# One tile of x1 moved from VectorE to GpSimd, a new order in the dense steps, and no wait for scatters in the edge steps

## The chip, the core and the metric

One core of a Trainium2 chip runs the whole kernel: TensorE (PE), VectorE (DVE), ScalarE (ACT), GpSimd (POOL) and SyncE (SP, used for its DMA queue). The metric is the time of one execution on the device in microseconds (us), less is better.

## The reference, cut to what matters

There are N = 50000 nodes with 128 features in `x`, and 12500 edges (98 tiles of 128 edges) sorted by destination.

```python
# layer 0 (GraphSAGE-like, max over edges)
pooled = relu(layer_norm((x[src] * (1 + softplus(coeff) * w[:, None])) @ pool_w + pool_b))
agg    = maximum(segment_max(pooled, dst), 0)
h      = relu(layer_norm(concat([x, agg]) @ final_w + final_b))
x1     = layernorm(x + h)
# layer 1 (relational graph convolution, 8 bases, mean over edges)
msg    = x1[src];  aggs[b] = segment_sum(msg * comp[edge_type][:, b], dst)
out    = concat([agg_b / max(deg, 1) for b], x1) @ weight + bias
return layernorm(x1 + out)
```

For a node without an incoming edge `agg` is zero, so its x1 and its output need its own row alone.

## The kernel before, in words

**Dense and edge groups.** A group is 4 tiles of 128 rows. The first 98 groups ("dense") are all rows of x: each gets x1 and an output as if it had no edges. Then 25 groups ("edge") redo the rows that are destinations of edges, with `agg`, and their x1 rows are scattered over the dense ones in `x1_table`. After that, phase C goes through the 98 tiles of edges in 25 units: it gathers x1 rows of the sources, multiplies by coefficients, applies the bases, sums by destination, normalises, and scatters the final rows into `out`.

**Steps.** A software pipeline of 130 steps, written out by hand on each engine. In step s a dense group g is at stage s - g: 0 load and transpose, 1 first matmul, 2 scaling by gamma, 3 beta and residual, 4 x1, 5 transpose of x1, 6 root matmul, 7 output. Beside it each step takes one tile of edges (from step 5 on) through gathers, a matmul and a running maximum (`scanned`), so that `agg` is ready for the edge groups. An engine does its stages of a step in program order; counting semaphores (`dve_x`, `act_x`, `pe_c`, ...) tie the engines together. Up to step 103 (`c < EDGE_ORDER`) one order holds, behind it another.

**VectorE in a dense step:** moments of the last statistics (L1084, L1085: two operands in SBUF), residual `h = max(h, 0) + x` (L1119: one instruction of 512 elements, both operands in SBUF, waits for `pool_b`), `spread` (L1090, waits for L1084), variance (L1095), bn_stats (L1107) four times, reciprocal (L1143), the scan (L1153), gamma scaling `scaled` (L1171, four times), the fourth tile of x1 (`first_layer`, L1202), `pooled_scaled` (L1164), the output (L1182).

**GpSimd in a dense step:** adds beta to the whole group (L461, waits for `dve_t`, that is for `scaled` of the step before), issues the gather of rows x[dst] (`gather_dst`, L431), scales the source rows by the edge's weight (`scale_src`, L452, 128x128), issues the gather of x[src] (`gather_src`, L438). In the edge steps it issues four scatters a group (L486).

**ScalarE in a dense step:** copy of x1 transposed (L775), square root of the reciprocals (`roots`, L782), squares of the root layer's output for its variance (`rooted`, L767), three tiles of x1 (`first_layer`, L805), squares of the first layer (`squares`, L767), the copy of the transposed rows (L827).

**TensorE in a dense step:** transposes of x1 (L539), root bias (L548), root matmuls (L554), first bias (L578), first matmuls (L586), transposes of rows (L565), the transpose of `pooled` (L600), the pooling layer (L610, L611). In `first_bias` it waits, in edge groups, until the scatters of the group five before have landed (`x1_scattered`): the brake of the diff below.

**SP's queue in a dense step** stores x_dst, loads the next group (after the residual), stores x1 (after `act_x` and `dve_x`), and stores the output.

Of the kernel before, what the change touches and what calls it, by code (L numbers as in the profile page):

```python
# [16 lines left out]
P = 128  # L17
CH = 4
# [55 lines left out]
def gnn_kernel(nc, x, src_cols, dst_cols, dst_next_cols, dst_rows, dst_prev_rows, type_line,  # L74
# [35 lines left out]
    with ExitStack() as ctx:  # L110
# [92 lines left out]
        def banks(a, n):  # L203
# [13 lines left out]
                 "dve_t", "dve_te", "pool_b", "apart_stored", "agg_ready", "act_e", "scaled", "e_ready", "dve_v", "dve_x", "act_x", "dve_o", "pe_c", "pe_cp", "act_c", "dve_scan", "pe_d",  # L217
# [71 lines left out]
        def _(sp):  # L289
# [44 lines left out]
            def step(s):  # L334
# [41 lines left out]
                if is_dense(c, 4):  # L376
                    sp.wait_ge(S["act_x"], s - 3)
                    sp.wait_ge(S["dve_x"], s - 3)
# [28 lines left out]
        def _(pool):  # L407
# [45 lines left out]

            def step(s):
# [17 lines left out]
                if is_tile(s, -3):  # L472
                    need(pool, S["pe_a"], s)
                    gather_src(s + 3 - LATE)
                if is_group(s, 4) and not is_dense(s, 4):
# [8 lines left out]
                    pool.wait_ge(S["dve_x"], s - 3)  # L484
# [39 lines left out]
        def _(pe):  # L524
# [3 lines left out]
            def step(s):  # L528
# [4 lines left out]
                def turned():  # L533
                    if is_group(c, 5):
                        pe.wait_ge(S["act_x"], s - 4)
                        pe.wait_ge(S["dve_x"], s - 4)
# [31 lines left out]
                def first_bias():  # L568
                    if c == 1:
                        pe.wait_ge(S["setup_dve"], 1)  # L570
                    if is_group(c, 1):
                        d = c - 1 - DENSE - LEAD
                        if d >= 0:
                            pe.wait_ge(x1_scattered[d % LEAD], 16 * CH * (d // LEAD + 1))
# [39 lines left out]
                if c < EDGE_ORDER:  # L614
                    turned()
                    root_bias()
                    rooted()
                    first_bias()
# [117 lines left out]
        def _(act):  # L736
# [25 lines left out]
            def step(s):  # L762
# [14 lines left out]
                def roots():  # L777
                    if 2 <= c <= GROUPS + 3:
                        act.wait_ge(S["dve_q"], s - 1)
                        if is_group(c, 5):  # L780
                            act.wait_ge(S["act_x"], s - 4)
                        nc.scalar.activation(st[:, 7, :], st[:, 6, :], ACT.Sqrt, scale=float(D)).then_inc(S["act_q"], 1)  # L782
# [58 lines left out]
                if c < EDGE_ORDER:  # L841
                    turned()
                    roots()
                    rooted()
                    first_layer()
# [49 lines left out]
        def _(dve):  # L895
# [202 lines left out]
            def step(s):  # L1098
# [24 lines left out]
                residual()  # L1123
                if stats:
                    own.need(first)
                    spread_at = spread(RES, TOP)

# [65 lines left out]
                def first_layer():  # L1193
                    if is_group(c, 4):
                        if is_dense(c, 4):
                            need(dve, S["pe_c"], s - 5)
                        else:
                            dve.wait_ge(S["pe_b"], s - 3)
                        if is_dense(c, 4) and is_dense(c, 6):
                            dve.wait_ge(x1_stored[b], 16 * since(c, 4 + b, 2))  # L1200
# [12 lines left out]
                if c < EDGE_ORDER:  # L1213
# [7 lines left out]
                    scaled()  # L1221
                    first_layer()
                    stats_of(2)
                    pooled_scaled()
# [145 lines left out]
```

## Time and profile before

| | |
|---|---|
| median of 3 runs | 882.5 us (880.93 to 883.58) |
| the profiled execution | 882.3 us, its span 880.5 us |
| busy share of the span | PE 90%, DVE 88%, ACT 68%, POOL 80% |
| TensorE's mean granted clock | 0.957 of full speed |
| dense steps | about 10 to 480 us of the span |
| edge steps | about 480 to 628 us |
| phase C | from 628 us |

The span runs from the first to the last instruction. A row of the trace gives start and duration of an instruction (or of several alike in a row, with xN), its line, what it writes and reads, and in brackets the idle time of its engine before it with what ended it ("issue": nothing that the profile shows). Starts can overlap the end of the instruction before, since the engines pipeline.

### The profile page before, as it was taken

How to read it: one execution, taken by the hardware profiler on the slowest of the kernel's cores; microseconds unless marked ns; L12 is line 12 of the kernel's file. 1: busy time of each engine (PE TensorE's matmuls, PEld its weight loads, DVE VectorE, ACT ScalarE, POOL GpSimd, SP SyncE). 2: the span in 40 equal slices, each digit the busy share in tenths (PEclk: the TensorE clock that was granted, in tenths of full speed). 3: DMA queues.
4: the chain of work that ended last, by engine and by line, in shares of the span. 5: the costliest groups of instructions: out<-in, count | busy, mean ns of one | idle time of the engine just before them, and what ended most of it. 6: DMA issues, size and time to landing. Idle time of an engine off the chain costs nothing.

```text
span 880.5 us, 17875 instructions
## 1 busy us (share of the span) xinstructions
PE 793.3 (90%) x4519; PEld 553.4 (63%) x4519; DVE 775.1 (88%) x2703; ACT 601.5 (68%) x2887; POOL 703.4 (80%) x703
## 2 busy tenths in 40 slices
PE   4699999999999999999999999997499998989760
PEld 3577777777777777777777787775345544434340
DVE  6999999999999999999999999986179999999780
ACT  4699999999999999999999988885202121111130
POOL 2599899899899899899898577776677777777777
PEclk9899999999999999999999999999589999999895
DMA  4366676666666666676666534444187887878711
GB/s 115 107 221 221 214 241 219 214 219 221 210 219 222 209 221 218 207 222 221 211 219 199 172 123 124 134 149 144 48 291 280 321 285 287 303 271 303 270 47 46
DMA packets 90699, 179.84 MB, mean 204 GB/s; under 512 B 17161, under 2 KB 36018, under 8 KB 84326
## 3 DMA queue, kind: packets, MB, share of 16 engines
q1 hardware_dynamic: 73414, 147.26, 50.1%
q0 software_dynamic: 15744, 30.96, 11.2%
q8 instruction: 37, 0.61, 0.3%
q10 hardware_dynamic: 1440, 0.50, 0.3%
q14 instruction: 64, 0.52, 0.2%
HBM read 109.02 MB, written 70.91 MB: 204 GB/s over the span
## 4 chain that ended last, share of the span: by engine, by line
PE 56%; POOL 23%; issue 9%; DVE 6%; ACT 3%; DMA 3%; ACTq 0%; POOLq 0%; DVEq 0%
PE ps L586 13%; PE ps L554 13%; POOL out_rows L431 11%; POOL rows L438 11%; PE ps L565 6%; PE ps L539 5%; PE ps L611 4%; PE ps L578 4%; PE ps L548 4%; PE ps L600 3%; PE ps L610 2%; POOL x_table L486 2%; PE ps L589 2%; DMA x_table<-agg_all,scat_x 1%; ACT junk L767 1%
## 5 line engine op out<-in xcount | busy, mean ns | idle before, releaser
L767 ACT ACTIVATE junk<-ps 128x128 bf16<-128x128 f32 x884 | 233.0, 287 | 21.1 <-PE ps L589 12.3
L767 ACT ACTIVATION_READ_ACCUMULATOR junk<-ps 128x1 f32 x884 | 193.6, 219 | 0.0
L719 PE MATMUL ps<-agg_all,w_cen 128*128 128x512 f32 (+1 forms) x400 | 178.0, 599 | 3.1 <-DVE agg_all L1271 2.5
L431 POOL DMA_INDIRECT x_dst<-in_x,dst_i x98 | 153.5, 1566 | 14.9 <-issue 4.5
L586 PE MATMUL ps<-w_cen,xT 128*128 128x128 f32 x984 | 157.8, 292 | 1.4 <-ACT xT L827 1.4
L461 POOL TENSOR_TENSOR work<-work,vec_raw 128x512 f32<-128x512 f32 x98 | 124.6, 1272 | 35.4 <-DVE work L1171 24.7
L586 PEld LDWEIGHTS ps<-w_cen,xT 128*128 128x128 f32 x984 | 127.9, 195 | 30.2 <-issue 27.9
L554 PE MATMUL ps<-w_cen,work 128*128 128x128 f32 x984 | 146.2, 293 | 0.0
L1271 DVE TENSOR_TENSOR agg_all<-coefs,ps 128x1024 f32<-128x1024 f32 x98 | 117.7, 1210 | 29.7 <-PE ps L705 18.3
L554 PEld LDWEIGHTS ps<-w_cen,work 128*128 128x128 f32 x984 | 122.3, 196 | 28.8 <-issue 28.8
L1107 DVE BATCH_NORM_STATS2 bn<-work 128x6 f32<-128x128 f32 x492 | 133.0, 276 | 0.7
L719 PEld LDWEIGHTS ps<-agg_all,w_cen 128*128 128x128 f32 x400 | 76.3, 196 | 88.5 <-issue 88.2
L486 POOL DMA_INDIRECT x_table<-agg_all,scat_x x98 | 94.2, 961 | 40.6 <-issue 27.4
L431 POOL DMA_INDIRECT out_rows<-work,scat_i x98 | 97.3, 993 | 29.9 <-issue 29.3
L438 POOL DMA_INDIRECT rows<-x_table,src_i x98 | 93.6, 955 | 31.8 <-issue 29.0
L438 POOL DMA_INDIRECT rows<-in_x,src_i x98 | 96.7, 987 | 18.7 <-issue 15.6
L1171 DVE SCALAR_TENSOR_TENSOR work<-ps,st,vec_raw 128x128 f32<-128x128 f32 x392 | 108.5, 336 | 2.2 <-ACT st L782 1.1
L881 ACT ACTIVATE st<-st 128x4 f32<-128x4 f32 x25 | 5.1, 206 | 148.2 <-DVE st L1307 147.8
L805 ACT ACTIVATE work<-work,st 128x128 f32<-128x128 f32 x294 | 97.9, 417 | 0.1
L565 PE MATMUL ps<-ident,rows 128*128 128x128 f32 x590 | 86.2, 276 | 7.6 <-DMA rows<-in_x 6.6
L827 ACT COPY xT<-ps 128x640 f32<-128x640 f32 (+1 forms) x123 | 85.7, 697 | 0.6 <-PE ps L565 0.6
L775 ACT COPY work<-ps 128x512 f32<-128x512 f32 x123 | 77.9, 633 | 1.7 <-PE ps L539 1.6
(147 smaller groups left out, 1399.8 us busy)
## 6 DMA issues: line engine op xcount, KB each, us to landing
coefs<-coef_line SPq DMA_DIRECT2D x49, 1024.0 KB, 7.4
rows<-in_x SPq DMA_DIRECT2D x97, 256.0 KB
x_table<-work SPq DMA_DIRECT2D x97, 256.0 KB, 2.1
out_rows<-outb SPq DMA_DIRECT2D x97, 256.0 KB, 2.1
x_dst_table<-x_dst SPq DMA_DIRECT2D x98, 64.0 KB
rows<-x_dst_table SPq DMA_DIRECT2D x24, 256.0 KB
apart<-apart_line SPq DMA_DIRECT2D x14, 224.0 KB
x_dst<-in_x,dst_i POOLq DMA_INDIRECT x98, 4.0
```

Source lines behind the costliest of these rows:

```text
L431: return pool.indirect_dma_start(*args, bounds_check=last_node, oob_is_err=False)
L438: return pool.indirect_dma_start(rows_of, None, table, by(columns, t))
L461: pool.tensor_tensor(h, h, vec_raw[:, BET_F:BET_F + 1, :].broadcast_to([P, CH, D]), ALU.add).then_inc(S["pool_b"], 1)
L486: pool.indirect_dma_start(x1_table[:, :], by(scat_x, d * CH + m), x1_tile(s - 4, m), None) \
L554: last = pe.matmul(Y[b][:, cols(m, m + 1)], x1T[:, b, m, :], w_cen[:, W_ROOT, :], start=False, stop=True, skip_group_check=True)
L565: last = pe.transpose(XT[:, cols(m, m + 1)], rows[:, slot, m, :], ident[:, :])
L586: last = pe.matmul(H[1 - b][:, cols(m, m + 1)], xT[:, 1 - b, m, :], w_cen[:, W_TOP, :], start=False, stop=is_dense(c, 1), skip_group_check ...
L719: last = pe.matmul(MT[b][:, 0:n * D], w_cen[:, W_BASE + m, :], prod[:, b, m, 0:n, :].rearrange("p t d -> p (t d)"), start=(m == 0), stop=( ...
L767: last = nc.scalar.activation(junk[:, kind * CH + m, :], bank[:, cols(m, m + 1)], ACT.Square, accum_out=power[:, b, 1, TOP + kind * CH + m ...
L1107: own.mark(dve.bn_stats(bn[:, RES + m, :], hn[:, (c - 3) % SLOTS, m, :]))
L1171: last = dve.scalar_tensor_tensor(hn[:, (c - 2) % SLOTS, m, :] if is_dense(c, 2) else h, h, st[:, 7, TOP + m:TOP + m + 1], vec_raw[:, GAM_ ...
L1271: dve.tensor_tensor(prod[:, b, half, two, :], coefs[:, p % COEF_SLOTS, :, half, :].rearrange("p t m d -> p m t d"), GX[c % len(GX)][:, col ...
```

## The change

1. `fourth_x1`, new on GpSimd: in dense steps tile 3 of x1 is made there, as a multiply of 128x128 by a broadcast column, behind `gather_src`; it signals `pool_x`. SP's store, TensorE's transposes and ScalarE's `roots` wait for `pool_x` in dense groups. VectorE's `first_layer` is left for edge groups alone, and `dve_x` counts only these.
2. Order in steps up to 103. TensorE: `first_bias` ahead of `rooted`. ScalarE: `first_layer` ahead of `rooted`. VectorE: the residual behind `spread` (this in all steps), and `pooled_scaled` ahead of `first_layer` and the third bn_stats.
3. TensorE's wait for `x1_scattered` in `first_bias` is gone.

```diff
@@ SP
-                    sp.wait_ge(S["dve_x"], s - 3)
+                    sp.wait_ge(S["pool_x"], s - 3)
@@ GpSimd
+            def fourth_x1(s):
+                c, b = s, s % 2
+                if is_dense(c, 4):
+                    pool.wait_ge(S["act_q"], s - 1)
+                    need(pool, S["pe_c"], s - 5)
+                    if is_dense(c, 6):
+                        pool.wait_ge(x1_stored[b], 16 * since(c, 4 + b, 2))
+                    pool.tensor_tensor(x1_tile(c - 4, X1_ACT), hn[:, (c - 4) % SLOTS, X1_ACT, :],
+                                       st[:, 7, RES + X1_ACT:RES + X1_ACT + 1].broadcast_to([P, D]), ALU.mult) \
+                        .then_inc(S["pool_x"], 1)
...
                     gather_src(s + 3 - LATE)
+                fourth_x1(s)
...
-                    pool.wait_ge(S["dve_x"], s - 3)
+                    pool.wait_ge(S["dve_x"], s - 3 - DENSE)
@@ TensorE
-                        pe.wait_ge(S["dve_x"], s - 4)
+                        if is_dense(c, 5):
+                            pe.wait_ge(S["pool_x"], s - 4)
+                        else:
+                            pe.wait_ge(S["dve_x"], s - 4 - DENSE)
...
-                        d = c - 1 - DENSE - LEAD
-                        if d >= 0:
-                            pe.wait_ge(x1_scattered[d % LEAD], 16 * CH * (d // LEAD + 1))
...
                     root_bias()
+                    first_bias()
                     rooted()
-                    first_bias()
                     first_layer()
@@ ScalarE
                         act.wait_ge(S["dve_q"], s - 1)
+                        if is_dense(c, 5):
+                            act.wait_ge(S["pool_x"], s - 4)
...
                     roots()
+                    first_layer()
                     rooted()
-                    first_layer()
                     squares()
@@ VectorE
-                residual()
                 if stats:
                     own.need(first)
                     spread_at = spread(RES, TOP)
+                residual()
...
-                    if is_group(c, 4):
-                        if is_dense(c, 4):
-                            need(dve, S["pe_c"], s - 5)
-                        else:
-                            dve.wait_ge(S["pe_b"], s - 3)
-                        if is_dense(c, 4) and is_dense(c, 6):
-                            dve.wait_ge(x1_stored[b], 16 * since(c, 4 + b, 2))
+                    if is_group(c, 4) and not is_dense(c, 4):
+                        dve.wait_ge(S["pe_b"], s - 3)
...
                     scaled()
+                    pooled_scaled()
                     first_layer()
                     stats_of(2)
-                    pooled_scaled()
                     stats_of(3)
```

## Rows read from the trace of the kernel before

**Rows 1.** Busy time by stretch: us; PE, PEld, DVE, ACT, POOL busy; clock; DMA
```profile
300.00:400.00 100.00, 98.72 (x657) 74.56 (x655) 96.85 (x383) 96.80 (x507) 89.99 (x86) 1.00 0.68 216
```

**Rows 2.** The chain of waits from 400 to 410 us: start, us, what
```profile
by line: PE ps L586 25.9%; PE ps L554 21.8%; PE ps L565 10.9%; PE ps L578 9.5%; PE ps L539 8.7%; PE ps L611 8.3%; PE ps L548 6.3%; PE ps L600 6.0%; PE ps L610 3.2%; issue 1.0%
...
404.55 0.32 PE ps L578
...
406.85 0.16 PE ps L610
```

**Rows 3.** GpSimd in order of time, at steps 12 and 98: start, us, engine, line
```profile
59.91 0.99 POOL L438 DMA_INDIRECT rows<-in_x,src_i  x1 [0.16 <-issue]
60.92 1.28 POOL L461 TENSOR_TENSOR work<-work,vec_raw 128x512 f32<-128x512 f32 x1
...
467.29 1.27 POOL L461 TENSOR_TENSOR work<-work,vec_raw 128x512 f32<-128x512 f32 x1
```

**Rows 4.** GpSimd and VectorE in order of time, one steady step
```profile
404.21 0.41 POOL L452 TENSOR_TENSOR rows<-rows,e_scale 128x128 f32<-128x128 f32 x1
...
404.77 0.99 POOL L438 DMA_INDIRECT rows<-in_x,src_i  x1 [0.16 <-issue]
...
405.72 0.27 DVE L1202 TENSOR_SCALAR work<-work,st 128x128 f32<-128x128 f32 x1
...
405.88 1.27 POOL L461 TENSOR_TENSOR work<-work,vec_raw 128x512 f32<-128x512 f32 x1
405.91 0.28 DVE L1107 BATCH_NORM_STATS2 bn<-work 128x6 f32<-128x128 f32 x1
...
407.30 1.59 POOL L431 DMA_INDIRECT x_dst<-in_x,dst_i  x1
407.30 0.68 DVE L1119 SCALAR_TENSOR_TENSOR work<-work,rows 128x512 f32<-128x512 f32 x1
...
408.19 0.47 DVE L1095 SCALAR_TENSOR_TENSOR st<-power,st 128x13 f32<-128x13 f32 x1
```

**Rows 5.** The same two engines in an early step, in order of time
```profile
46.93 1.28 POOL L461 TENSOR_TENSOR work<-work,vec_raw 128x512 f32<-128x512 f32 x1
...
47.93 0.31 DVE L1084 TENSOR_TENSOR st<-bn 128x4 f32<-128x4 f32 x1
...
48.25 0.69 DVE L1119 SCALAR_TENSOR_TENSOR work<-work,rows 128x512 f32<-128x512 f32 x1
48.37 1.46 POOL L431 DMA_INDIRECT x_dst<-in_x,dst_i  x1 [0.16 <-issue]
```

**Rows 6.** The same, in step 6 and in an edge step
```profile
32.78 1.02 POOL L431 DMA_INDIRECT x_dst<-in_x,dst_i  x1 [0.17 <-issue]
...
33.29 0.69 DVE L1119 SCALAR_TENSOR_TENSOR work<-work,rows 128x512 f32<-128x512 f32 x1
33.89 0.16 DVE L1090 SCALAR_TENSOR_TENSOR st<-st 128x4 f32<-128x4 f32 x1
...
34.15 0.17 DVE L1095 SCALAR_TENSOR_TENSOR st<-power,st 128x13 f32<-128x13 f32 x1
...
552.41 0.96 POOL L486 DMA_INDIRECT x_table<-agg_all,scat_x  x1 [0.30 <-issue]
552.44 0.43 DVE L1029 TENSOR_TENSOR w_cen<-w_cen,row_mean 128x256 f32<-128x256 f32 x1
```

**Rows 7.** Waits from 495 to 630 us (total us, times, longest), and one scatter
```profile
POOL x_table L486 <- DVE agg_all L1202: 8.5, 7, 3.6
...
PEld ps L578 <- DMA x_table<-agg_all,scat_x: 5.0, 3, 3.9
...
608.29 0.96 POOL L486 DMA_INDIRECT x_table<-agg_all,scat_x  x1 [3.60 <-DVE agg_all L1202]
```

**Rows 8.** Phase C on GpSimd: its first gather, and the gathers as a group
```profile
628.47 0.98 POOL L438 DMA_INDIRECT rows<-x_table,src_i  x1 [2.24 <-DMA x_table<-agg_all,scat_x]
...
L438 POOL DMA_INDIRECT rows<-x_table,src_i x98 | 93.6, 955 | 31.8 <-issue 29.0
```

More of the change, by code:

```diff
@@ L216, in gnn_kernel @@
                  "setup_dve", "bases_dve", "base_sums", "bases_ready", "soft_dve", "soft_act", "pe_a", "act_a", "pe_b", "pe_e", "act_h", "dve_q", "act_q",
-                 "dve_t", "dve_te", "pool_b", "apart_stored", "agg_ready", "act_e", "scaled", "e_ready", "dve_v", "dve_x", "act_x", "dve_o", "pe_c", "pe_cp", "act_c", "dve_scan", "pe_d",
+                 "dve_t", "dve_te", "pool_b", "apart_stored", "agg_ready", "act_e", "scaled", "e_ready", "dve_v", "dve_x", "pool_x", "act_x", "dve_o", "pe_c", "pe_cp", "act_c", "dve_scan", "pe_d",
                  "act_y", "act_o", "dve_own", "deg_dve", "deg_pe", "root_centred", "col_sums", "root_ready", "c_own", "pe_g", "act_g",
```

## The prediction

> **What bounds the kernel now.** I read the stretches first. Through the dense steps TensorE, VectorE and ScalarE are each busy 97 to 99% of the time and GpSimd 90%, all at the full TensorE clock [rows 1]. Then the chain of waits for two steps: TensorE's own instructions from end to end, with 1% of "issue" [rows 2]. The spacing of the beta addition on GpSimd (L461) gives the period: from step 12 (60.92 us) to step 98 (467.29 us) [rows 3] there are 86 steps in 406.4 us, 4.725 us each. Then one step in order of time [rows 4]. It shows that four loops close at nearly the same length:
> - TensorE: 4.72, of which 0.05 is "issue" (1.0% of 10 us, two steps) [rows 2]; it lies just before L600, the transpose that needs VectorE's `pooled`.
> - ScalarE: 3.2% idle [rows 1], so 4.58 of work and 0.15 of gaps.
> - GpSimd, back to back: L461 1.27, gap 0.15, L431 1.59, gap 0.03, L452 0.41, gap 0.16, L438 0.99, gap 0.02 [rows 3, 4] = 4.62.
> - VectorE with GpSimd: scaled, then L461, then the residual L1119, then statistics, then scaled again.
>
> After the dense steps the bound is GpSimd's issue of indirect DMAs. Scatters take 0.96 us each with 0.30 between; of their waits, 8.5 us in 7 places are for VectorE's x1 [rows 7]. From the first gather of phase C (628.47) on, GpSimd issues 98 gathers and 98 scatters with about 0.30 us between them [rows 8], 252 us that begin when the last x1 row has landed. So the end moves by what the dense and edge steps give or take.
>
> **The change, part by part.**
>
> *The fourth tile on GpSimd.* VectorE loses L1202: from its start to that of the next instruction 0.19 us (405.72 to 405.91). GpSimd gains one multiply of 128x128 with a broadcast column, the form of L452: 0.41 us, plus 0.02 for the gap as between L438 and L461. It stands behind L438, and ahead of the next L461. Its inputs are there when its turn comes (L438 ends at 405.76): L1202 needed the same three semaphores and ran at 405.72. It would be ready near 406.2. Those who wait for it are the store on SP's queue (with the output store, the copy of x_dst and the next load behind it), TensorE's transposes of the next step, and ScalarE's next root, ahead of which the change adds a wait; all of them come after the next L461 has started (405.88), and before, the store waited for ScalarE's three tiles, which end later than L1202. So each costs nothing as long as GpSimd keeps pace. A price for the three waits isn't shown; bounds are 0 (L461's gap of 0.02 behind a wait) and 0.16 (the gap before L438, which waits too); I take 0, the nearest row being a vector operation like it. As the rows of before stand GpSimd would then need 4.62 + 0.43 = 5.05 us a step, more than 4.72. The question is therefore whether the 1.59 us of L431 stay.
>
> *Why L431 takes 1.59 us.* The same gather took 1.02 us at 32.78, where the residual L1119 started 0.51 us after it; at 48.37, where L1119 had started 0.12 us before it, 1.46; in the steady steps both start within 0.01 us and it takes 1.59 [rows 4 to 6]. In each slow case it ends 1.58 to 1.59 us after L1119's start: it waits out L1119 (two operands in SBUF) and then does its whole work. I counted 94 gathers slowed so, and none where L1119 started more than 0.01 us after L431. Rows of L1119 starting between 0.01 and 0.51 after don't exist.
>
> *The new order of VectorE.* The residual moves behind L1084, L1085 and the spread L1090, which waits for L1084. Without L1202, VectorE reaches L1084 0.19 us earlier, while L461 still runs, and is held there: at 47.93 L1084 took 0.31 instead of 0.15, and ended 0.03 after L461 (48.21) [rows 5]. From its end a dependent instruction needs 0.10 to 0.14 us (L1090 ends 34.05, L1095 starts 34.15 [rows 6]), and the next one follows 0.07 later. So, counted from the end of L461, L1090 starts at 0.13 to 0.17 and L1119 at 0.20 to 0.24, while L431 starts at 0.15: L1119 comes 0.05 to 0.09 us after L431, where before it came with it. Does L431 get through? For: the scatter L486 at 552.41, with a two-operand VectorE instruction starting 0.03 after it, took its plain 0.96 [rows 6]. Against: L1090, also with two operands, starts at L431's own time, and L1119 follows it closely. I take "gets through": L431 1.02, so GpSimd's floor is 4.62 - 0.57 + 0.43 = 4.48 us, and it is not the bound. The other end is a full stall: L431 ends 0.22 + 1.59 after L461, GpSimd's floor is 1.27 + 1.81 + 0.03 + 0.41 + 0.16 + 0.99 + 0.02 + 0.41 + 0.02 = 5.12.
>
> The page "SBUF — State Buffer" of the Trainium skill (section "SBUF: two separate sides") says that the port pair which VectorE and GpSimd share is an exclusive lock, that a VectorE operation with two SBUF inputs contends for it against a GpSimd operation that reads SBUF, and that whoever starts first keeps it for the whole instruction while the other blocks. The stalls above agree with the first two. The last would have L431, once first, hold L1119 up for its whole length; the row at 33.29 speaks against that (L1119 took 0.69 in the middle of a gather), but it makes a rival below.
>
> *What is then late next.* VectorE's loop through L461 is 4.72 now. L1119 would come 0.07 later behind L461 (0.22 for 0.15), but L1095 sooner behind L1119: 0.60 (33.29 to 33.89) instead of 0.86 (to 34.15) [rows 6]: 4.53. And L1095 took 0.47 at 408.19 beside the stalled gather, 0.17 at 34.15 [rows 4, 6]: if that goes too, 4.23. TensorE: `pooled` comes right behind scaled, ahead of two instructions it stood behind, so L600's 0.05 goes; the two bias matmuls now stand side by side. A bias matmul of 512 columns (L578) is 0.32 of the chain, one of 128 columns (L610) 0.16 [rows 2], so 384 columns are 0.16, and some 0.11 of each is not columns; side by side saves 0 to 0.11, and TensorE's floor is 4.56 to 4.67. ScalarE: 4.58 plus gaps that may stay (0.04 to 0.11), as its order only swaps two blocks. I take 4.65 for the period, bounds 4.58 and 4.69. Sum: 86 x (4.65 - 4.725) = -6.5 us, between -12.5 and -3.
>
> *No brake in the edge steps.* TensorE's first bias waited for scatters 5.0 us in 3 places, the longest 3.9 [rows 7]; it is followed by GpSimd's wait of 3.60 at 608.29 and one of 0.87 later. Less the 0.30 that any gap has, these two are 3.9 us. The other 1.1 us of the brake come before; they shorten GpSimd's later waits by as much. Together -5.0. ScalarE makes the x1 of the first edge group ahead of its four squares instead of behind them, which may bring the first scatter forward by up to 1.0, the four squares' time; I take half. Bounds: -1 (another engine paces those steps) and -6.4 (all of 8.5 less 7 x 0.30). Taken -5.5. The clock dips to half in the idle stretches around 600 and 620 us; the first would go too, inside the same sum.
>
> *Sum.* -6.5 - 5.5 = -12.0 against the profiled execution's own 882.3 us (span 880.5), which is 0.2 under the median of 882.5: 870.4 us.
>
> **The rivals.**
> 1. *L431 still stalls behind the residual* (slower). Place: every dense step. Price: 5.12 - 4.725 = 0.395 x 86 = +34.0, some +2 in steps 5 to 12, -5.5 at the edge: 912.8, give or take 5. It decides as soon as GpSimd's floor passes 4.7, that is when more than about a third of the steps stall. For: the distance is under 0.1 us and L1090 sits on L431's start. Against: 552.41.
> 2. *A part of the steps stalls*, or the three waits of the new tile cost their 0.16 each: GpSimd's period between 4.70 and 5.0, so 876 to 900.
> 3. *The gather holds the residual.* By that page's rule, worked out in this kernel: L1119 would start at L431's end (1.17 after L461), VectorE's loop is 4.23 to 4.53 and 0.95 more: 5.18 to 5.48, dense +39 to +65, time 916 to 942. Against it: L1119 at 33.29, and L1029 at 552.44, which took 0.43 us beside a scatter.
> 4. *The dense steps don't move* (another loop stands at 4.72) and only the brake counts: 877.
>
> **How the numbers follow.** Forecast, with 4: 0.57. Rival 1: 0.23. Rival 2: 0.15. Rival 3: 0.05. About 0.3% (2.6 us) can be told from no change. Faster: 0.57 and half of rival 2 = 0.65. Same: 0.06. Slower: 0.29. The likeliest case's own range is 865 to 879. The range of 8 in 10 has to reach over rival 2 into rival 1: 865 to 911.
>
> **What would show it.** Right: L461 spaced 4.6 to 4.7; L431 near 1.02 us with L1119 starting 0.05 to 0.09 after it; L1084 stretched to L461's end; the new multiply 0.41; L600 without a wait; no wait of L578 for a scatter; the last scatter less than 1.0 us late after the one before. Wrong: L431 of 1.6 us or more and a GpSimd that is busy without a gap, period 5.1; then rival 1. A residual that takes over 1 us is rival 3. A period of 4.72 with TensorE's chain unbroken says that the bias matmuls and L600 gave nothing.

## The result, and the profile after

The changed kernel takes 861.86 us (median of 3 runs, 861.31 to 862.27), the kernel before 882.5: ratio 0.9767, interval 0.9742 to 0.9793. A second series later gave 861.71 against 882.79. The forecast was 870.4 with a range of 865 to 911: the direction was right, the gain is 20.6 us where 12.0 were expected, and the time lies below the range. The profiled execution's span is 860.5 us, 20.0 less than before (clock 0.956, before 0.957).

Where the 20.0 us come from, by landmarks on GpSimd (the beta addition, L461 before and L472 now; the scatters, L486 and L498; the first gather of phase C, L438):

| stretch | before | after | difference | forecast |
|---|---|---|---|---|
| start to step 12 | 60.92 | 60.23 | -0.7 | - |
| steps 12 to 98 (86 steps) | 406.37 | 388.23 | -18.1 | -6.5 |
| step 98 to step 100 | 10.01 | 10.24 | +0.2 | - |
| step 100 to the first scatter | 17.69 | 18.77 | +1.1 | -0.5 |
| first scatter to phase C | 133.48 | 131.01 | -2.5 | -5.0 |
| phase C | 252.0 | 252.0 | 0 | 0 |

The steps that answer to [rows 3]; from them the period is 388.23 / 86 = 4.514 us (before 4.725):

```profile
60.23 1.27 POOL L472 TENSOR_TENSOR work<-work,vec_raw 128x512 f32<-128x512 f32 x1
...
448.46 1.27 POOL L472 TENSOR_TENSOR work<-work,vec_raw 128x512 f32<-128x512 f32 x1
```

The stretch from 300 to 400 us, columns as in [rows 1]:

```profile
300.00:400.00 100.00, 96.84 (x688) 75.03 (x688) 96.74 (x377) 99.24 (x535) 91.21 (x111) 1.00 0.73 227
```

Before, TensorE stood highest with 98.7%; now ScalarE does, with 99.2%. The chain of waits from 400 to 410 us, which was all TensorE's [rows 2], now has no piece of it:

```profile
by line: ACT junk L779 41.5%; ACT work L819 19.8%; ACT xT L841 17.5%; ACT junk L831 12.1%; ACT st L796 6.0%; ACT work L787 4.6%; issue 4.4%; ACTq L53 0.5%
```

And a steady step on GpSimd and VectorE, to lay beside [rows 4] (L1098, L1104, L1133 and L1109 are the old L1084, L1090, L1119 and L1095; L461 is now the new multiply):

```profile
403.37 1.28 POOL L472 TENSOR_TENSOR work<-work,vec_raw 128x512 f32<-128x512 f32 x1
...
404.45 0.23 DVE L1098 TENSOR_TENSOR st<-bn 128x4 f32<-128x4 f32 x1
...
404.71 0.17 DVE L1104 SCALAR_TENSOR_TENSOR st<-st 128x4 f32<-128x4 f32 x1
...
404.79 0.72 DVE L1133 SCALAR_TENSOR_TENSOR work<-work,rows 128x512 f32<-128x512 f32 x1
404.79 1.04 POOL L431 DMA_INDIRECT x_dst<-in_x,dst_i  x1
...
405.66 0.17 DVE L1109 SCALAR_TENSOR_TENSOR st<-power,st 128x13 f32<-128x13 f32 x1
...
407.42 0.42 POOL L461 TENSOR_TENSOR work<-work,st 128x128 f32<-128x128 f32 x1
```

The gather took 1.04 us where it took 1.59, although the residual starts with it again, at 404.79, as it did before. The variance behind it took 0.17 where [rows 4] had 0.47, and the new multiply 0.42.

### The profile page after: what moved, and what is told of

Read it like the earlier page. It is cut to its first block, busy times and chain, and to the rows that moved or that the text cites. A ratio compares the mean times of both kernels' runs of the same rounds, so it can differ in the third digit from the quotient of the medians.

```text
span 860.5 us, 17875 instructions
## 1 busy us (share of the span) xinstructions
PE 767.1 (89%) x4519; PEld 542.2 (63%) x4519; DVE 756.1 (88%) x2605; ACT 593.2 (69%) x2887; POOL 692.1 (80%) x801
## 4 chain that ended last, share of the span: by engine, by line
DVE 31%; POOL 23%; ACT 22%; issue 11%; PE 10%; DMA 2%; DVEq 0%; SPq 0%; ACTq 0%; POOLq 0%
POOL out_rows L431 11%; POOL rows L438 10%; ACT junk L779 9%; DVE work L1185 7%; ACT work L819 5%; DVE bn L1121 5%; DVE work L1133 4%; DVE outb L1196 4%; ACT xT L841 3%; PE ps L569 2%; PE ps L598 2%; ACT junk L831 2%; PE ps L601 2%; ACT st L796 2%; DVE agg_all L1167 2%
## 5 line engine op out<-in xcount | busy, mean ns | idle before, releaser
L779 ACT ACTIVATE junk<-ps 128x128 bf16<-128x128 f32 x884 | 227.7, 280 | 11.7 <-PE ps L601 9.1
L779 ACT ACTIVATION_READ_ACCUMULATOR junk<-ps 128x1 f32 x884 | 189.4, 214 | 0.0
L569 PEld LDWEIGHTS ps<-w_cen,work 128*128 128x128 f32 x984 | 122.8, 196 | 47.7 <-issue 46.9
L598 PE MATMUL ps<-w_cen,xT 128*128 128x128 f32 x984 | 150.8, 286 | 0.6 <-ACT xT L841 0.6
L569 PE MATMUL ps<-w_cen,work 128*128 128x128 f32 x984 | 146.8, 294 | 0.0
L472 POOL TENSOR_TENSOR work<-work,vec_raw 128x512 f32<-128x512 f32 x98 | 124.6, 1271 | 22.3 <-DVE work L1185 19.5
L598 PEld LDWEIGHTS ps<-w_cen,xT 128*128 128x128 f32 x984 | 131.4, 199 | 7.4 <-issue 5.5
L1121 DVE BATCH_NORM_STATS2 bn<-work 128x6 f32<-128x128 f32 x492 | 126.1, 277 | 3.6 <-DVE work L1133 0.9
L498 POOL DMA_INDIRECT x_table<-agg_all,scat_x x98 | 94.1, 960 | 37.9 <-issue 27.5
L438 POOL DMA_INDIRECT rows<-x_table,src_i x98 | 93.6, 955 | 31.8 <-issue 29.6
L431 POOL DMA_INDIRECT x_dst<-in_x,dst_i x98 | 102.4, 1045 | 14.4 <-issue 2.3
L1185 DVE SCALAR_TENSOR_TENSOR work<-ps,st,vec_raw 128x128 f32<-128x128 f32 x392 | 110.3, 344 | 2.8 <-ACT st L796 1.8
L438 POOL DMA_INDIRECT rows<-in_x,src_i x98 | 96.7, 987 | 18.3 <-issue 15.7
```

What stands on the lines that cost most here:

```text
L431: return pool.indirect_dma_start(*args, bounds_check=last_node, oob_is_err=False)
L438: return pool.indirect_dma_start(rows_of, None, table, by(columns, t))
L472: pool.tensor_tensor(h, h, vec_raw[:, BET_F:BET_F + 1, :].broadcast_to([P, CH, D]), ALU.add).then_inc(S["pool_b"], 1)
L569: last = pe.matmul(Y[b][:, cols(m, m + 1)], x1T[:, b, m, :], w_cen[:, W_ROOT, :], start=False, stop=True, skip_group_check=True)
L598: last = pe.matmul(H[1 - b][:, cols(m, m + 1)], xT[:, 1 - b, m, :], w_cen[:, W_TOP, :], start=False, stop=is_dense(c, 1), skip_group_check ...
L779: last = nc.scalar.activation(junk[:, kind * CH + m, :], bank[:, cols(m, m + 1)], ACT.Square, accum_out=power[:, b, 1, TOP + kind * CH + m ...
```

## The experiments

Two theories on the dense steps. **A**: the stalled gather was what mattered; it frees GpSimd for the new multiply, and everything that puts the residual ahead of the gather costs that back. **B**: TensorE never bound at 4.725; what bounds after the change is ScalarE, and the orders of TensorE and ScalarE are worth little. For the edge steps: the brake was worth the held scatters, or it was cover for something else.

Four of them (`e_residual`, `e_pe_order`, `e_act_order`, `e_brake`) ran on one chip on which everything behind the dense steps is slower (the kernel before took 971.6 us there, 966.35 to 976.92; from the first scatter to phase C it is 182 to 184 us there, on the others 129 to 136). So of them only ratios and the dense steps are used; these had their usual pace there. The changed kernel itself did not run on that chip. Kernels with the same dense steps (the two runs of the changed one, `e_brake`, `e_brake_again`, `e_edge_residual`) have periods from 4.514 to 4.527, so 0.01 us of period means nothing. On the others the kernel before took 882.8 to 883.4.

**e_residual**: residual back ahead of the spread, in dense steps.
```diff
+                if c < EDGE_ORDER:
+                    residual()
                 if stats:
                     own.need(first)
                     spread_at = spread(RES, TOP)
-                residual()
+                if c >= EDGE_ORDER:
+                    residual()
```


> The changed kernel with VectorE's residual back ahead of the spread in the dense steps (the edge steps keep the new order). Theory A (what frees GpSimd's gather of x_dst is that the residual no longer follows the two moments directly): the gather takes 1.46 to 1.6 us again, GpSimd's floor is 4.93 to 5.07, +0.42 to +0.56 us a step, +36 to +48 us, 898 to 910. Theory B (VectorE, freed of the fourth tile, is early enough in any order): the gather stays at 1.04 and the time within 2 us of 861.9.

982.89 us, ratio 1.0133 (1.0061 to 1.0205), period 4.887. The residual starts 0.12 us ahead of the gather, which takes 1.49:

```profile
302.84 0.69 DVE L1133 SCALAR_TENSOR_TENSOR work<-work,rows 128x512 f32<-128x512 f32 x1
302.96 1.49 POOL L431 DMA_INDIRECT x_dst<-in_x,dst_i  x1 [0.16 <-PE ps L554]
303.45 0.16 DVE L1104 SCALAR_TENSOR_TENSOR st<-st 128x4 f32<-128x4 f32 x1
303.74 0.44 DVE L1109 SCALAR_TENSOR_TENSOR st<-power,st 128x13 f32<-128x13 f32 x1
```

With the extra multiply GpSimd now sets the period: its five instructions follow each other after 1.44 + 1.51 + 0.57 + 1.01 + 0.36 = 4.89 us (medians), none of them with a wait for another engine. One line moved costs 0.37 us a step against the changed kernel (4.887 for 4.514), nearly twice what the whole change gained.

**e_tile_alone**: the kernel before with only the tile moved to GpSimd (old orders, brake); cut to the call.
```diff
                     gather_src(s + 3 - LATE)
+                fourth_x1(s)
```


> The kernel before with the fourth tile on GpSimd and nothing else: old orders, brake kept. Both theories: the residual starts 0.12 us before the gather, which takes 1.46 to 1.5 us; GpSimd needs 1.27 + 0.15 + 1.48 + 0.03 + 0.41 + 0.16 + 0.99 + 0.02 + 0.41 + 0.03 = 4.95 us a step, so +0.2 x 86 = +19 us against the kernel before. If VectorE is late instead and the gather gets through, the period is 4.5 to 4.7.

897.92 us, ratio 1.0167 (1.0147 to 1.0187), period 4.877, gather 1.49: the same picture on the ordinary chip. This is the first rival's mechanism, at +13 us in the dense steps (86 x 0.152) and not +34.

**e_resid_only**: the kernel before with the residual behind the spread, nothing else.
```diff
-                residual()
                 if stats:
                     own.need(first)
                     spread_at = spread(RES, TOP)
+                residual()
```


> The kernel before with one line moved: VectorE's residual behind the spread (the fourth tile stays on VectorE, the brake and all other orders stay). Theory A (the old bound of 4.725 us was the loop of GpSimd and VectorE with the gather stalled behind the residual; TensorE only kept step with it): the gather drops to about 1.04 and the period to 4.5 to 4.6, which is -11 to -19 us. Theory B (TensorE bounded the steps at 4.72 and its bias order had to change too): the gather drops, the period stays at 4.65 to 4.72, at most -6 us.

870.85 us, ratio 0.9858 (0.9839 to 0.9877), period 4.580. The gather takes 1.02, the residual starts 0.12 after it. So this single move gives 12.5 of the 18.1 us of the dense steps (86 x 0.145). TensorE is busy 99.75% here:

```profile
300.00:400.00 100.00, 99.75 (x679) 77.27 (x679) 97.12 (x395) 97.62 (x523) 80.43 (x88) 1.00 0.71 221
```

That is not its floor. The transpose of `pooled` (L600) starts 0.68 us after the five transposes ahead of it (median, 0.54 to 0.96), where in `e_pe_order` below, with the same order on TensorE, 0.56 is enough for a step of 4.52. One of these steps, with 0.70:

```profile
403.24 0.71 PE L565 MATMUL ps<-ident,rows 128*128 128x128 f32 x5
403.94 0.30 PE L600 MATMUL ps<-ident,pooled 128*128 128x128 f32 x1
```

ScalarE's squares wait for TensorE's L554 (2.3 us in 100) and VectorE's variance for ScalarE's L817 (2.5), so that the three wait for each other in turn. Which link would have to give for less than 4.58 was not tested.

**e_order_alone**: the new orders and no brake, the fourth tile left on VectorE, behind `pooled_scaled`; cut to VectorE's part.
```diff
                     scaled()
+                    pooled_scaled()
                     first_layer()
                     stats_of(2)
-                    pooled_scaled()
                     stats_of(3)
```


> The changed kernel with the fourth tile made by VectorE again: new orders on all engines, no brake. Theory A (GpSimd's own work of 4.51 us bounds the changed kernel): GpSimd falls to 4.07 and the period follows the next engine, VectorE at about 4.55 (4.37 busy and 0.19) or ScalarE at 4.48: between 4.48 and 4.6, within 3 us of the changed kernel or up to 7 us slower. Theory B (the tile on GpSimd is what brings the gain): period back near 4.7, +17 us against the changed kernel.

954.17 us, ratio 1.0805 (1.0784 to 1.0826), period 5.579: much slower, which I had not expected. The cause is one instruction:

```profile
300.15 1.26 POOL L461 TENSOR_TENSOR work<-work,vec_raw 128x512 f32<-128x512 f32 x1 [1.28 <-DVE work L1168]
300.24 1.25 DVE L1199 TENSOR_SCALAR work<-work,st 128x128 f32<-128x128 f32 x1
```

The tile on VectorE (L1199) starts 0.09 us after the beta addition and takes 1.25 us instead of 0.28 (0.27 to 0.28 in every other kernel that has it there): it is held until the addition ends. All that VectorE has to do behind it comes a microsecond late.

**e_tile_first**: the same, but the tile directly behind the four scalings, so that it starts ahead of the addition.
```diff
                     scaled()
-                    pooled_scaled()
                     first_layer()
+                    pooled_scaled()
                     stats_of(2)
```


> The changed kernel with the fourth tile on VectorE directly behind the scaling (as before), pooled behind it; the other new orders stay, no brake. Tests why the same order with the tile behind pooled took 5.58 us a step. Theory A (behind pooled it starts 0.09 us after GpSimd's beta addition and is held until its end, 1.25 us for 0.28; directly behind scaled it starts ahead of it): the tile takes 0.28 again, period 4.5 to 4.6, whole time 860 to 869. Theory B (VectorE can't carry the tile in the new order whatever its place): period over 5, above 900.

861.65 us (860.52 to 862.25), ratio 0.9751 (0.9728 to 0.9775), period 4.514. The same tile now starts ahead of the addition and takes its plain time:

```profile
403.13 0.28 DVE L1199 TENSOR_SCALAR work<-work,st 128x128 f32<-128x128 f32 x1
...
403.29 1.27 POOL L461 TENSOR_TENSOR work<-work,vec_raw 128x512 f32<-128x512 f32 x1 [0.48 <-DVE work L1168]
```

It is as fast as the change, with GpSimd at 82% instead of 91%. Moving the tile to GpSimd is therefore one way to keep it out of the addition's way, and not the source of the gain. Against `e_resid_only` (4.580) this kernel has the new orders of TensorE and ScalarE and `pooled_scaled` ahead of the third bn_stats: together they are the remaining 0.066 us a step.

**e_pe_order** and **e_act_order**: TensorE's, then ScalarE's old order in the changed kernel.
```diff
                     root_bias()
-                    first_bias()
                     rooted()
+                    first_bias()
```


> The changed kernel with TensorE's old order (root matmuls ahead of the first bias). Theory A (TensorE was the bound at 4.72 us a step and its floor fell by some 0.2 because the two bf16 bias matmuls now share one switch; GpSimd and ScalarE at 4.51 bound the steps now): the floor returns to about 4.65, so +0.14 x 86 = +12 us, 874, with TensorE at 99% busy. Theory B (TensorE was never the bound, the old chain only ran through it): within 1 us of 861.9, period 4.51.

```diff
                     roots()
-                    first_layer()
                     rooted()
+                    first_layer()
```


> The changed kernel with ScalarE's old order (squares of the root layer ahead of x1). Theory A (ScalarE is a bound now at 99% busy and the new order took 0.1 us of its gaps and waits out of a step): period up by 0.05 to 0.1 and +4 to +9 us, 866 to 871. Theory B (the order of two blocks on ScalarE is worth nothing where GpSimd alone is the bound): within 1 us of 861.9; x1 comes 1.0 us later and the store with it, which nobody waits for.

949.31 (ratio 0.9798, 0.9733 to 0.9862) and 946.99 (0.9774, 0.9703 to 0.9845); periods 4.526 and 4.497. With its old order TensorE is busy 99.88% of the time at 4.526 us a step. So the work that before filled 4.725 us fits into 4.526, and no effect of its new order on the period can be told from the spread of like kernels. Theory B, for the kernel with the tile on GpSimd.

**e_pool_light** and **e_act_light**: less work on one engine. In the first, GpSimd scales one column of 128 of the source rows (L452, tiles 4 to 89); in the second ScalarE leaves one of the four squares of the root layer out in steps 12 to 97. These parts of the computation are missing.
```diff
-                pool.tensor_tensor(r, r, e_scale[:, t:t + 1].broadcast_to([P, D]), ALU.mult).then_inc(S["scaled"], 1)
+                w = 1 if 4 <= t < 90 else D
+                pool.tensor_tensor(r[:, 0:w], r[:, 0:w], e_scale[:, t:t + 1].broadcast_to([P, w]), ALU.mult).then_inc(S["scaled"], 1)
```


> The changed kernel; GpSimd's scaling of source rows works on 1 column instead of 128 for edge tiles 4 to 89, so part of that result is left out. It frees some 0.26 us of GpSimd a step, floor 4.25. Theory A (GpSimd's 4.51 alone bounds the step): the period falls to ScalarE's 4.48 or a little above it, -0.02 to -0.03, -2 us. Theory B (GpSimd isn't the bound): 4.51 stays. If VectorE and GpSimd together made the 4.51, it falls below 4.45.

```diff
-                        squared(Y[b], 1).then_inc(S["act_y"], 1)
+                        squared(Y[b], 1, CH - 1 if 12 <= c < 98 else CH).then_inc(S["act_y"], 1)
```


> The changed kernel with one of ScalarE's four squares of the root layer left out in steps 12 to 97, 0.25 us of ScalarE a step, so the variance of a fourth of those rows is left out. Theory A (GpSimd bounds): period 4.51, unchanged. Theory B (ScalarE, 99% busy, bounds): the period falls to below 4.45, -5 us or more.

860.91 (0.9745, 0.9717 to 0.9773) and 854.2 (0.9669, 0.964 to 0.9698); periods 4.513 and 4.441. GpSimd is not the bound, ScalarE is. Relieved, it hands over after 0.07 us, to VectorE, which has no idle time left:

```profile
300.00:400.00 100.00, 98.51 (x696) 76.00 (x697) 100.00 (x383) 97.59 (x498) 91.81 (x113) 1.00 0.74 230
```

GpSimd has no slack there either: its own five spacings add up to 1.43 + 1.07 + 0.57 + 1.01 + 0.36 = 4.44. Which of the two stops at 4.44 these runs don't tell.

**e_nudge**: the kernel before with one more small addition on VectorE between L1085 and the residual, its result unused.
```diff
                 own.mark(dve.tensor_tensor(power[:, par, 1, a:b], bn[:, a:b, 2], bn[:, a:b, 5], ALU.add))
+                own.mark(dve.tensor_tensor(st[:, 3, a:b], bn[:, a:b, 2], bn[:, a:b, 5], ALU.add))
```


> The kernel before with one more small addition on VectorE (128x4, the form of L1085, its result unused) between L1085 and the residual: the residual starts some 0.06 to 0.10 us later, and what stands ahead of it is still a two-operand instruction of the kind that stood there. Theory 'only the distance counts: a gather that has begun is let through': the gather takes 1.02 to 1.05, the period 4.58 to 4.65, the time 870 to 876, although an instruction was added. Rival 'what stands ahead of the residual counts (in the kernel after the spread, in before the moments)': the gather still takes 1.5 to 1.6 and the time is 882 to 890.

899.22 us, ratio 1.0183 (1.0162 to 1.0204), period 4.881. Half of each theory: the gather takes 1.02, the residual starting 0.12 after it, so the distance does decide there; but the time is neither's. The step got 0.156 us longer, although GpSimd got 0.57 us back:

```profile
400.18 0.15 DVE L1085 TENSOR_TENSOR power<-bn 128x4 f32<-128x4 f32 x1
400.26 0.18 DVE L1086 TENSOR_TENSOR st<-bn 128x4 f32<-128x4 f32 x1
400.36 0.68 DVE L1120 SCALAR_TENSOR_TENSOR work<-work,rows 128x512 f32<-128x512 f32 x1
400.97 0.37 DVE L1091 SCALAR_TENSOR_TENSOR st<-st 128x4 f32<-128x4 f32 x1
401.46 0.28 DVE L1096 SCALAR_TENSOR_TENSOR st<-power,st 128x13 f32<-128x13 f32 x1
```

The two small instructions behind the residual are stretched (0.37 and 0.28), as one of them was in [rows 4] (L1095, 0.47). VectorE has no waits in such a step. So in the kernel before it was VectorE that set the period, and its loss beside the gather is the same whether the gather gets through or not. Theory A in its plain form ("a free gather is the gain") falls with this run. What the new order gains, by the spacings in the table below, is that the spread is no longer behind the residual.

**e_brake**, **e_brake_again** (the changed kernel with the brake, on the slow and on an ordinary chip) and **e_no_brake** (the kernel before without it).
```diff
                     if is_group(c, 1):
+                        d = c - 1 - DENSE - LEAD
+                        if d >= 0:
+                            pe.wait_ge(x1_scattered[d % LEAD], 16 * CH * (d // LEAD + 1))
                         need(pe, S["dve_t"], s - 2)
```


> The changed kernel with TensorE's wait for scatters put back in the edge steps; nothing else. Theory A (read from the two traces: the last 28 scatters follow back to back now, where before there were 3.3 + 0.57 us of gaps behind the brake's 3.9 us hold): +3.9 us, so about 866, with the hold of nearly 4 us back at the fourth last group. Theory B (the dense steps' end and not the brake set the edge steps' time, the brake is worth nothing): within 1 us of 861.9. My prediction's term of 5.0 to 5.5 us would give 867.

954.32, ratio 0.9816 (0.9752 to 0.988); period 4.527. No run on that chip differs from it by the brake alone, so it says nothing on the brake.

> The kernel after with TensorE's wait for x1_scattered back in first_bias, once more, on a chip where the edge steps may run at their usual speed. Theory 'the brake cost what the two held waits show' (3.60 and 0.87 us less 0.30 each in the trace of before, none of it in the trace of after): 3 to 5 us slower than the kernel after, so 865 to 867. Rival 'another engine paces those steps, the brake was cover for VectorE's x1': within 1 us of it, 861 to 863. Dense period 4.51 in both.

865.74 us (864.93 to 866.1), ratio 0.980 (0.978 to 0.982).

> The kernel before with that wait left out and nothing else changed. By the first theory 3 to 5 us under the kernel before, 878 to 880; by the rival within 1 us of it. Dense period 4.725 in both, and the first scatter where before had it.

879.48 us, ratio 0.9956 (0.9939 to 0.9974). The brake costs 865.74 - 861.7 = 4.0 us in the one and 883.41 - 879.48 = 3.9 in the other, and 4.0 to 4.1 in both by the stretch from the first scatter to phase C (135.10 against 131.0; 133.48 against 129.43). The waits from 470 to 612 us; first the changed kernel with the brake, where GpSimd waits 4.7 us longer for VectorE's x1:

```profile
POOL x_table L498 <- DVE agg_all L1214: 15.1, 11, 4.1
...
PEld ps L593 <- DMA x_table<-agg_all,scat_x: 5.0, 3, 3.8
```

and the changed kernel:

```profile
POOL x_table L498 <- DVE agg_all L1211: 10.4, 9, 4.1
```

**e_edge_residual** and **e_tile_first_act**, looking for a better version: the old place of the residual in edge steps (the code below), and `e_tile_first` with ScalarE's old order.
```diff
+                if c >= EDGE_ORDER:
+                    residual()
                 if stats:
                     own.need(first)
                     spread_at = spread(RES, TOP)
-                residual()
+                if c < EDGE_ORDER:
+                    residual()
```


> The changed kernel with the old order of residual and spread in the edge steps alone (from step 104). Theory A (there the spread's wait for its moments stands in VectorE's way for 0.1 to 0.15 us in every step that VectorE bounds, and TensorE's first bias waits for the residual): up to -2 us in 25 steps, 860. Theory B (edge steps are bound by TensorE and the scatters): within 0.5 us of 861.8.

> The new order without the brake, the fourth tile on VectorE directly behind the four scalings (which took 861.65), and ScalarE in its old order (which gave a period of 4.497 where the kernel after has 4.514). If ScalarE's order is worth that here too, 86 x 0.017 = 1.5 us: 860.2, less what a later first edge group costs (up to 1.0). If the fourth tile's place matters more, no change from 861.7.

861.34 us (859.77 to 862.73; 0.9745, 0.9718 to 0.9772) can't be told from the change. The other took 870.36 (0.9845, 0.9822 to 0.9869), period 4.605: ScalarE's old order, which in `e_act_order` gave 4.497, costs 0.09 a step here. So the orders are worth little only with the tile on GpSimd. Why it is so was not settled. ScalarE waits there for L554 (1.9 us in 100) and VectorE for ScalarE's L814 (2.0), neither of which `e_tile_first` has.

**after_again**: the changed kernel once more, beside `e_resid_only`.

> The changed kernel as it is, as the reference for the runs beside it: period of the dense steps 4.51 us, gather of x_dst 1.04 us, whole time 0.977 of the kernel before.

861.71 us, ratio 0.9756 (0.9737 to 0.9775), period 4.514. No version beats the change by more than its uncertainty, except the one that leaves work out.

## Why the prediction was right and wrong

**What bounds: the step that failed.** It said that four loops close near 4.72 us and took TensorE for the first of them. Busy shares of 97 to 99% fitted each. Only VectorE had no slack; GpSimd's beta addition came 0.12 us behind the gather and not 0.02, being released by VectorE's `scaled`, and TensorE waited for VectorE's `pooled`. The wait stood just before L600, where I saw it, but as 0.05 us. The rows of before show the start of L600 0.75 us after that of L565:

```profile
405.80 0.71 PE L565 MATMUL ps<-ident,rows 128*128 128x128 f32 x5
406.55 0.30 PE L600 MATMUL ps<-ident,pooled 128*128 128x128 f32 x1
```

In `e_pe_order`, with the same order of TensorE and no such wait, it is 0.56:

```profile
404.15 0.71 PE L580 MATMUL ps<-ident,rows 128*128 128x128 f32 x5
404.71 0.30 PE L612 MATMUL ps<-ident,pooled 128*128 128x128 f32 x1
```

Five transposes have a modelled length of 0.71 in both, so that most of the wait lay under the modelled end. Over the steady steps the medians are 0.77 and 0.56: the wait was 0.21 us. TensorE's floor in its old order was 4.52 (`e_pe_order`: 4.526 at 99.88%) and not the 4.67 from which I worked, so the bounds of the period rested on 0.15 us that weren't there. Nor was the chain of waits a proof that TensorE bound: from 300 to 400 us of `e_act_order` it is TensorE's from end to end too (2.9% "issue"), at a period of 4.497, where TensorE could do its work in 4.22 (below).

**ScalarE: the term that was mis-sized.** I took 96.8% x 4.725 = 4.57 (4.58 in the prediction) for its work, plus gaps. Worked out alike, 99.24% x 4.514 = 4.48, and the gaps are 0.03. The same instructions are recorded shorter: the squares 281 against 290 ns, the three x1 tiles 391 against 418 each (stretches of 100 us of both kernels). They don't follow each other any faster: a square and its read take 0.25 us from start to start in both kernels, the three tiles 0.88 and 0.89. What shrank is a wait: the square root (L782, L796 after) starts 0.73 us after the start of the copy ahead of it before and 0.48 after, while the copy's recorded length is 0.65 and 0.66 (medians). The rows of one step before, then of one after:

```profile
403.59 0.65 ACT L775 COPY work<-ps 128x512 f32<-128x512 f32 x1
404.31 0.21 ACT L782 ACTIVATE st<-st 128x13 f32<-128x13 f32 x1
```
```profile
401.36 0.66 ACT L787 COPY work<-ps 128x512 f32<-128x512 f32 x1
401.84 0.29 ACT L796 ACTIVATE st<-st 128x13 f32<-128x13 f32 x1
```

So ScalarE's slack before was 0.25 us and not 0.15, and a busy share multiplied by the period is no floor of an engine's work. These two errors, both on the high side, put the forecast at 4.65 with bounds 4.58 to 4.69, where 4.514 came: 86 x 0.136 = 11.7 us. That is more than the whole miss of 8.5; the difference went back at the edge, below.

**VectorE's loop: right within the bounds.** I had 4.53, or 4.23 if the stretched variance got its plain time. In `e_act_light`, where VectorE waits for nothing, it is 4.44. The variance did become plain (0.17 at 405.66), but where ScalarE doesn't hold the step, it is stretched again. The spacings of VectorE in the median of some 48 steps show where it gained (all other instructions between: before 3.30, of which L1202 is 0.19, in `e_act_light` 3.11):

| from the first of the moments to | before | e_nudge | e_resid_only | e_act_light |
|---|---|---|---|---|
| the residual | 0.15 | 0.26 | 0.28 | 0.39 |
| the variance | 1.04 | 1.36 | 1.01 | 1.05 |
| behind the variance | 1.43 | 1.56 | 1.18 | 1.33 |

**The gather gets through: right, its reason wrong.** 1.04 us instead of 1.59 came, but not the distance of 0.05 to 0.09. L1084 (now L1098) was stretched to the end of the addition, as said; L1104 followed 0.03 after L1098's end and not 0.13, so the residual starts -0.02 to 0.00 from the gather, where by my rule it should have stalled. `e_resid_only`, `e_nudge` and `e_tile_first` have +0.12 to +0.13 and 1.02; `e_residual` and `e_tile_alone` have -0.12 and 1.49. Between them lies a tie that the records, to 0.01 us, don't resolve: before 0.00 (-0.01 to 0.01) and 1.59, `e_no_brake` +0.01 and 1.59, after -0.01 and 1.04. What decides in a tie is open. The forecast was lucky here.

**GpSimd's floor: right within 0.04.** 4.48 was forecast. The spacings of after add up to the period (1.42 + 1.08 + 0.57 + 1.01 + 0.44 = 4.51), but the last, from the new multiply to the next addition, is 0.36 in `e_residual`, `e_tile_alone` and `e_act_light`: 0.08 of it is a wait for VectorE, and the floor is 4.44. `e_pool_light` shows too that GpSimd doesn't set the period.

**The multiply and its three waits: right**, 0.41 us and nothing measurable (`e_tile_first` has neither and takes the same time). I missed what the move was worth in this order: left behind `pooled_scaled`, the tile would have run under the beta addition at a loss of 92 us (954.17 - 861.7).

**TensorE's order: the term was too small.** I had 0 to 0.11, a floor of 4.56 to 4.67; TensorE itself gained 0.30. By medians of the spacing in steady steps, the first of the two bias matmuls, now side by side, is followed after 0.23 us where each was followed after 0.31, the eight root matmuls after 0.99 (1.09) and the eight first matmuls after 0.89 (1.00):

```profile
404.89 0.39 PE L563 MATMUL ps<-root_bias,ones 3*128 3x512 bf16 x1
405.12 0.37 PE L590 MATMUL ps<-bias,ones 3*128 3x512 bf16 x1
405.43 1.16 PE L569 MATMUL ps<-w_cen,work 128*128 128x128 f32 x8
406.42 1.06 PE L598 MATMUL ps<-w_cen,xT 128*128 128x128 f32 x8
407.31 0.71 PE L580 MATMUL ps<-ident,rows 128*128 128x128 f32 x5
```

With 0.56 ahead of the transpose of `pooled` that is a floor of 4.22, from 4.52. The period shows none of it, since other engines bound; the transpose just waits longer than before (0.84 in place of 0.56), where I had forecast no wait.

**The brake: mechanism right, size off.** The two held waits were priced at 3.9 us, and 3.9 to 4.1 were measured. The 1.1 us that I added for its earlier, shorter waits didn't come: the longer gaps between scatters ahead of the two held ones are the same with the brake (0.60, 0.60, 0.95, 0.94, 0.55, 1.47 us before) and without it (0.61, 0.60, 0.94, 0.95, 0.57, 1.45 in `e_no_brake`). Nor did the half microsecond at the start: the profiled execution lost 1.1 there. That part is the execution's, not the kernel's. TensorE's clock fell to half for some 3.4 us (columns as in [rows 1]):

```profile
466.00:467.40 1.40, 0.67 (x4) 0.46 (x5) 1.38 (x6) 1.40 (x3) 0.00 (x0) 1.00 0.83 263
467.40:470.80 3.40, 3.40 (x19) 3.40 (x18) 3.25 (x12) 2.42 (x13) 1.86 (x3) 0.52 0.55 146
```

In `after_again` it stayed at 1.00 there, and the stretch from step 100 to the first scatter is 17.14 instead of 18.77, 0.55 less than before: so the first scatter does come half a microsecond forward when the clock holds. It doesn't reach phase C. From the first scatter on, the changed kernel needs 131.0 where `e_no_brake` needs 129.4, and from step 100 to phase C `after_again` takes 148.2 and `e_no_brake` 147.1. Of the 1.6 us `e_edge_residual` gives back 0.6 (130.4); the rest is open.

**Rival 1**: 912.8 was too dear. Its period is 4.88 (`e_tile_alone`), not 5.12: the gather, with the residual 0.12 ahead, ends 0.15 + 1.49 after the addition and not 0.22 + 1.59, which is 0.17 less, and the multiply with its gap takes 0.36 where 0.43 was put; together 0.24. **Rival 2** did not come: the gather took 1.04 to 1.05 in every steady step, and the three waits cost nothing measurable. **Rival 3** stays without support: the residual took 0.68 to 0.73 in every kernel whose gather ran beside it. In `e_order_alone` it took 0.91, but there it starts behind the gather's end and lies beside the scaling of the source rows (L452). **Rival 4** is refuted: the dense steps moved by 18.1 us.

## What to carry to other kernels

When all engines are 97 to 99% busy, find the one whose instructions start at their plain spacing with no wait, and take TensorE's spacing from a run in which it surely does not wait, not from its modelled ends: a wait of 0.21 us was seen as 0.05. Put instructions that VectorE and GpSimd contend for on the early side of the other engine's long instruction; a shift of 0.2 to 0.3 us in start was worth 92 us here. And test each part of a change by itself: 12.5 of the 18 us in the dense steps came from one line, and the part that gave the change its name was replaceable.

## What the runs showed of the hardware

- A one-input VectorE instruction in 32 bits (tensor_scalar, 128x128, both sides in SBUF) that starts 0.09 us after a GpSimd tensor_tensor is held for its whole rest (1.25 us for 0.28), and one that starts 0.16 us ahead of it is not. The Trainium skill, "SBUF — State Buffer", section "SBUF: two separate sides", says of a VectorE operation in a 2-port mode and one on GpSimd that whichever starts first has the shared port pair for the whole instruction and the other blocks. The held tile agrees; that it runs in such a mode no trace shows. The other way round the rows show no block: with the tile 0.16 us ahead, the addition takes its 1.27 us and starts 0.08 us behind the scalings, as with the tile behind it (1.26, 0.08). The issue of an indirect DMA doesn't hold a residual (two operands in SBUF) that starts in its middle either: that takes its plain 0.68 us.
- Small two-operand VectorE instructions beside such an issue are stretched, by up to 0.3 us (L1095 0.47, L1091 0.37), with or without a stall of the gather.
- Eight f32 matmuls of 128x128 in a row are followed 1.09 us after their start when a bf16 bias matmul stands on both sides (L554 before), after 0.99 to 1.00 with one on one side (L586 before, L569 after) and after 0.89 with none (L598 after). These are medians in steady steps at the full clock. Two bias matmuls side by side leave one group with none.
- TensorE's clock fell from 2.4 to 1.2 GHz for some 3.4 us in one profiled execution and not in another of the same kernel (467.4 to 470.8 us, granted 0.52 with TensorE busy all the while; just before, it had been busy for 0.67 of 1.40 us at the full clock, waiting 1.00 us for the residual). In the other, whose steps lie 0.38 us earlier, it had been busy for the same 0.67 of 1.40 behind the same wait (465.62 to 467.02), so what TensorE did just before doesn't explain the difference. Two more executions with the same dense steps have the fall (`e_brake` and `e_edge_residual`, granted 0.53 to 0.62 between 468 and 472 us). The stretch from step 100 to the first scatter was 1.6 us longer with the fall.
